# A short awaited GpSimd memset behind every gather of three graph layers

## The reference

```python
edge_index = jnp.stack([src, dst])
x = x + _L0_gnn_ref(_layernorm(x), edge_index, W, a)        # first graph layer
#   h = x @ W; e = exp(-leaky_relu(s[src] + t[dst])); out = relu(segment_sum(e * h[dst], src) / rowsum)
x = x + _L0_ffn_ref(...)
x = x + _L1_gnn_ref(_layernorm(x), edge_attr_8, edge_attr_4, ..., edge_index)   # second
#   gathers rows of a table by dst, products with edge weights, segment_sum by src
x = x + _L1_ffn_ref(...)
x = x + _L2_gnn_ref(_layernorm(x), src, dst, Wq, Wk, Wv, ...)   # third
#   logits = sum(Q[dst] * K[src]); softmax over the edges of each dst; segment_sum(V[src] * w, dst)
x = x + _L2_ffn_ref(...)
x = x + _L3_gnn_ref(_layernorm(x), W, att, src, dst)            # fourth
#   e = leaky_relu(es[src] + ed[dst]); softmax over the edges of each dst; segment_sum(alpha * z[src], dst)
x = x + _L3_ffn_ref(...)
```

## Time and profile before

| | us |
|---|---|
| median of 3 runs | 4805.37 |
| lowest and highest run | 4794.99, 4830.16 |
| the profiled execution, its span | 5525.9 |

### The profile page before, as it was taken

How to read it: one execution, slowest core, us unless ns; L and a number is a source line. 1 busy time by engine, 2 the same in 40 slices (tenths; PEclk the granted TensorE clock), 3 DMA queues, 4 the chain that set the end, 5 groups by cost and what they waited for, 6 DMA issues and landing times. The chain is left out here.

```text
span 5525.9 us, 74396 instructions
## 1 busy us (share of the span) xinstructions
PE 3832.4 (69%) x19148; PEld 2554.7 (46%) x19148; DVE 3300.9 (60%) x8316; ACT 2731.0 (49%) x8902; POOL 2677.9 (48%) x2640
## 2 busy tenths in 40 slices
PE   6916888722529999978566666668999936656565
PEld 2415566512414444457434444445556524444454
DVE  7913788723427999876557777764333425555653
ACT  5903667621217888854235555553233326656621
POOL 5876566664257777605325555532000046766234
PEclk8957899855758999989778888889999967777778
DMA  3013233312313333422435555540000033333334
GB/s 116 23 24 86 76 79 83 77 19 64 121 37 87 89 89 90 84 69 68 123 113 146 147 141 144 146 109 1 6 12 12 10 88 85 86 85 84 32 111 131
DMA packets 278822, 441.38 MB, mean 80 GB/s; under 512 B 114083, under 2 KB 192781, under 8 KB 278157
## 3 DMA queue, kind: packets, MB, share of 16 engines
q0 software_dynamic: 124624, 331.70, 23.6%
q1 hardware_dynamic: 147230, 98.37, 6.2%
q10 hardware_dynamic: 6560, 6.55, 0.4%
HBM read 368.84 MB, written 67.60 MB: 79 GB/s over the span
## 5 line engine op out<-in xcount | busy, mean ns | idle before, releaser
L2501 PE MATMUL PB<-XNT 128*128 128x260 f32 x1760 | 630.3, 500 | 61.0 <-DVE XNT L2475 48.1
L2620 POOL DMA_INDIRECT bigt<-ZTAB,DO x440 | 461.4, 1049 | 273.4 <-issue 125.0
L1002 POOL DMA_INDIRECT bigt<-HTAB,bigt x440 | 454.2, 1032 | 269.0 <-ACT bigt L1094 143.0
L355 POOL DMA_INDIRECT RECS<-bigt x391 | 471.7, 1206 | 166.7 <-issue 102.0
L1955 POOL DMA_INDIRECT bigt<-YTAB,bigt x440 | 474.9, 1079 | 139.0 <-issue 127.0
L2620 POOL DMA_INDIRECT bigt<-KVTAB,DO x296 | 282.0, 953 | 356.5 <-DVE XNT L2383 191.4
L2501 PEld LDWEIGHTS PB<-XNT 128*128 128x128 f32 x1760 | 389.2, 244 | 130.8 <-DVE XNT L2383 57.0
L700 ACT ACTIVATE bigt<-bigt 128x128 f16<-128x128 f16 x1214 | 374.8, 389 | 96.3 <-DVE bigt L673 45.5
L1983 PE MATMUL PB<-bigt 128*128 128x512 f32 x880 | 400.7, 597 | 3.0 <-DVE bigt L2170 3.0
L709 PE MATMUL PB<-bigt 128*128 128x440 f16 x1564 | 354.6, 370 | 27.0 <-ACT bigt L700 12.8
L2053 ACT ACTIVATE bigt<-bigt 128x64 f32<-128x64 f32 x1320 | 327.6, 334 | 90.8 <-issue 48.4
(11 more groups left out here) (490 smaller groups left out, 9836.3 us busy)
## 6 DMA issues: line engine op xcount, KB each, us to landing
bigt<-YTAB,bigt POOLq DMA_INDIRECT x552
bigt<-SRT SPq DMA_DIRECT2D x56, 128.0 KB
OUTS<-bigt SPq DMA_DIRECT2D x56, 128.0 KB
SRT<-bigt SPq DMA_DIRECT2D x11, 640.0 KB, 10.3
bigt<-HTAB,bigt POOLq DMA_INDIRECT x440
bigt<-ZTAB,DO POOLq DMA_INDIRECT x440
KVTAB<-bigt SPq DMA_DIRECT2D x25, 258.0 KB
YTAB<-bigt SPq DMA_DIRECT2D x10, 640.0 KB, 10.6
```

The source lines that it names most:

```text
L355: e.indirect_dma_start(out=RECS, out_offset=bass.IndirectOffsetOnAxis(ap=APOS[:, c:c + 1].bitcast(U32), axis=0), in_=ATTR[:, piece % 2, k, ...
L1002: e.indirect_dma_start(out=Gt[:, g % GB, j, :], out_offset=None, in_=HTAB, in_offset=bass.IndirectOffsetOnAxis(ap=SO[:, g * G + j:g * G + ...
L2501: m = e.matmul(self.PV[n % len(self.PV)], self.OH[:, g % 2, j, :], self.msg[:, g % 2, j, :], start=(k == 0), stop=(k == self.H - 1))
L2620: e.indirect_dma_start(out=dst[:, j, :], out_offset=None, in_=table, in_offset=bass.IndirectOffsetOnAxis(ap=DO[:, g * G + j:g * G + j + 1] ...
```

## The change

Behind each gather of L1002 and of L2620 POOL writes zeros over one partition of `iotai` (128 int32 numbers) and waits until that is done, before it goes on. That is 440 memsets and waits in each of three layers, 1320 in all. Nothing else is changed; the second graph layer has none.

```diff
@@ -357,6 +357,13 @@
+        lull = iotai[0:1, :]
+
+        def pause(e):
+
+            e.memset(lull, 0).then_inc(Q.up(), 1)
+            e.wait_ge(*Q.now())
+
@@ -1003,6 +1010,7 @@
                             in_offset=bass.IndirectOffsetOnAxis(ap=SO[:, g * G + j:g * G + j + 1].bitcast(U32), axis=0),
                         ).then_inc(gathered.sem(g), 16)
+                        pause(e)
```

## The result

| | us |
|---|---|
| before, median of 5 runs | 4813.80 (4794.99 to 4830.16) |
| after, median of 5 runs | 4971.29 (4954.92 to 5044.95) |
| ratio after/before | 1.0312 (95% interval 1.0277 to 1.0348) |
| profiled execution after, its span | 5043.1 |

The changed kernel is 3.1% slower; the medians are 157 us apart. The ratio leaves out the two slow ones of the five runs after, 5039.80 and 5044.95 us, which the median of the table has in it.

A forecast was written before the change was run, and what follows sets the result against it. In the three changed loops the consumers set the pace and POOL has slack. Pauses are hidden except at the starts, 2.4 + 3.2 + 1.6 = 7 us, about 6 on the median of 4805.37: 4812 us, range 4710 to 4990.

The forecast's parts named there:

- The price of a pause: On POOL, from gather to gather: 1.46 us instead of 1.26, so 0.20 us more for each memset with its wait.
- The far bound of 1.04 us: Highest price considered per added memset, from a copy between gathers with other engines at full work: 2.30 us instead of 1.26.
- What of it is hidden: In the three loops, 88 us of added POOL work each fits into POOL's idle time of 143, 276 and 115 us.
- break-even: Price per pause that uses up POOL's idle time: 0.33 us in the first layer, 0.63 third, 0.26 fourth.
- the first rival: In the three loops, pauses cost more than POOL's idle time covers: 4963 to 4987 us at 0.50 us each; chance 0.33.
- The starts: Loop beginnings, before the ring of buffers is full, pay for pauses: 2.4 + 3.2 + 1.6 = 7 us.
- The price over the slack: In the three loops, pauses exceed POOL's idle time, deciding from 0.26 us each; 4963 to 4987 us at 0.50; chance 0.33.
- Held-up signals let through: In the three loops, pauses shrink VectorE's 170 us of stalls: 4731 us if half goes, 4657 if all; chance 0.20.
- the second rival: Pauses in the stream of gathers release signals VectorE waits for in the three loops: 4731 or 4657 us; chance 0.20.
- The pause isn't one: On POOL, the memset runs beside the unfinished gather, so nothing changes: 4805 us; shares the main forecast's chance of 0.47.
- Contention: On SBUF ports shared with VectorE: a memset only writes, so it is priced as in the quiet stretch, not 1.04 us.

## Why the prediction was right and where it was wrong

The time, 4971.29 us, lies in the range of 4710 to 4990, but not where I expected it. The forecast was 4812 us and no measurable change; it came out 3.1% slower. That it lies in the range is owed to its upper end, which had been drawn for a rival with a chance of 0.33, and that rival's sum, 4963 to 4987 us for a pause of 0.50 us, comes near the measured time by luck: the pause cost 0.16. By its steps:

**The price of a pause** was right: 0.20 us taken, 0.16 measured. The memset took 0.19 us as the larger one of the earlier trace rows, began at the gather's end as the copy of the earlier trace rows did, and the gather behind it waited 0.27 us where the earlier trace rows has 0.24. The far bound of 1.04 us played no part. It was also misread: 0.72 us of it was a gather that lasted 1.68 us in place of 0.96, and not the copy.

**What of it is hidden** is the step that failed. I set 88 us against a slack of 143, 276 and 115 us. In the timed condition the slack was 0, 63 and 0 us. With those numbers my own break-even would have been 0, 0.14 and 0 us a pause, below the price in every loop. The slack was read rightly; it belongs to the late condition, in which POOL waits for a ring whose users get their signals late, and the sum mixed it with a median of the prompt one.

The text had the warning in it, 5525.9 us against 4805.37. It names it in favour of the first rival, and its last line calls it what would make the forecast wrong most easily, but the slack in the sum stayed as it was. Small amounts were divided by 1.15, the lengths of the loops were not. Divided, they are 628, 707 and 610 us, while POOL's gathers as they are in that profile and 439 gaps of 0.30 make 586, 551 and 593. That leaves 42, 156 and 17 us of slack, and pauses of 88 us a loop, my own price, would have cost 46 + 71 = 117 us, or 4922 us; at the measured price, 73 us a loop, it is 31 + 56 = 87 us, or 4892. Both are still too little, but over 1% slower.

**The starts** (7 us) can't be told apart, since all of a loop is paid and not its start only.

**The price over the slack**, the first rival, is what happened, by its other argument: not a price of 0.50 us or more, but a slack that the shorter runs don't have. It was said to decide from 0.26 us on. It decided from nothing on in two loops.

**Held-up signals let through**, the second rival, did nothing in the timed runs: no profile of that condition has a late signal. In the late condition it is what happens, at 0.974 of the time; I had worked out 4731 and 4657 us, which are 0.985 and 0.969 of 4805. My reason against it, that a pause of half a microsecond is too short, didn't hold. That the pause is a gap through which a signal slips, as the rival has it, isn't shown either: with pauses the waits end during gathers about as often as by chance.

**The pause isn't one** falls with the spacing of 1.42 us.

**Contention.** I expected none for a memset, and it took its 0.19 us in all loops: 1320 of them with a mean of 195 ns. What I left out is that the pauses change how many of the gathers are long, which was worth 48 us less in the first loop and 20 more in the fourth. In the fourth VectorE's product has a part in them; why the first loop has so few no run shows.

## What to carry to other kernels

Compare the span of a profiled execution with the timed runs before reading slack from it. If it is much longer, its idle time may not exist in the runs that count; add up what the engine must do (here 440 gathers and their gaps) against the stage's length scaled to the timed runs, or take another profile. Here a pause took 0.16 us of POOL's time, and the three loops lost 0.06 to 0.23 us a gather by it in the timed runs. In this kernel it paid only where other engines' signals arrived late.

## What the runs showed of the hardware that I had not expected

**A machine condition that turns the sign of a change.** The kernel before took 4810 to 4819 us in some comparisons and 5432 to 5434 in others, 13% apart, and the same edit gave 1.031 in one and 0.974 in the other. The mark of the late condition in a profile is the "remote" waits: 655 us on VectorE and 643 on ScalarE in before, none in the prompt one.

**Scatters held for many microseconds.** Before its first gather POOL issues 190 scatters (L355), while VectorE builds tables in half precision without a break. POOL's timeline of after at that place, and VectorE's:

```profile
201.16 7.68 POOL L355 DMA_INDIRECT RECS<-bigt  x1 [0.30 <-issue]
209.14 7.66 POOL L355 DMA_INDIRECT RECS<-bigt  x1 [0.30 <-issue]
217.11 35.03 POOL L355 DMA_INDIRECT RECS<-bigt  x1 [0.30 <-issue]
...
210.69 0.87 DVE L695 TENSOR_SCALAR bigt<-iotah,bigt 128x440 f16<-128x440 f16 x3
211.43 0.47 DVE L692 TENSOR_TENSOR bigt<-bigt 128x256 f16<-128x256 f16 x1
```

One scatter lasted 35.03 us, and VectorE ran 109 instructions in that time without an idle moment. In the nine profiles of the prompt condition the first gather of the first layer comes 295 to 296 us plus what its 190 scatters last over 0.96 us: 31 us in the kernel with pauses in the first layer only (first gather at 326.0), 77 in the kernel before (373.1), 125 in after (420.2). It is also why after's profile, at 5043.1 us, is so long, and probably why its median is 4971.29 and why the runs of one kernel scatter by up to 90 us: the 125 - 31 = 94 us between the profiles are as much, but the timed runs without a profile don't show their scatters. The loops' lengths are free of it, and so the experiments are judged by them.

The Trainium skill, "SBUF — State Buffer", section "Who interferes with whom", says that VectorE in a two-port mode contends with GpSimd, and that whichever issues first gets the shared ports "for the whole instruction", while the other fully blocks. That VectorE blocks GpSimd agrees with this row, whose instructions may be of that mode (the trace doesn't say, and no run took them away); but the hold lasted over 109 VectorE instructions, not one. The same section says that a VectorE instruction with two SBUF inputs holds up only a GpSimd instruction that reads SBUF, and infers from other DMAs that generating their descriptors isn't held by it. A gather takes its 128 indices from SBUF. With the product of two SBUF inputs (L2391) short, the long gathers of the fourth loop fell from 81 to 35 in the late condition, and from 54 to 48 without pauses in the prompt one. That agrees with the rule if a gather counts as an instruction that reads, and not with the inference if it is applied to gathers.
